# A fused attention and mixture-of-experts layer: the seam between its two halves, with a separate fp16 list of the rows and the last chunks' work reordered

## The reference

```python
xn = _layernorm(x, axis=-1)                       # x: 4 x 1024 x 256, that is 4096 rows
x  = x + attn(xn, w_attn, w_proj) + ffn(xn, ...)

# attn: causal linear attention, 16 heads of 16, chunks of 128 rows, phi = elu + 1
scores = where(mask, q_c @ k_c.T, 0)
num = scores @ v_c + q_c @ S ;  den = scores.sum(-1) + q_c @ z
S = S + k_c.T @ v_c ;  z = z + k_c.sum ;  y = num / (den + 1e-6) ;  return y @ w_proj.T

# ffn: each row goes to one of 8 experts
top_idx = argmax(xn @ gate_w.T + gate_b + expert_bias)
out = relu(xn @ w1[e] + b1[e]) @ w2[e] + b2[e]    # e = top_idx of the row
```

## Time and profile before

| | |
|---|---|
| median of 3 runs | 510.94 us (509.48 to 511.06) |
| profiled execution | 512.02 us |
| its span, first to last instruction | 510.2 us |
| mean granted TensorE clock | 0.992 |
| busy: PE, DVE, ACT, POOL | 486.4, 389.6, 280.7, 307.3 us |
| first `g1` matmul | 287.25 us from the start |

### The profile page before, as it was taken

The page is one execution under the profiler, slowest core; times in us unless marked ns, Lnnn a source line. Parts: engine busy times, 40 slices in busy tenths (PEclk is TensorE's granted clock), DMA queues, the critical chain, the costliest instruction groups (busy, mean ns, idle before and its releaser), DMA issues.

```text
span 510.2 us, 17893 instructions
## 1 busy us (share of the span) xinstructions
PE 486.4 (95%) x6293; PEld 403.4 (79%) x6293; DVE 389.6 (76%) x849; ACT 280.7 (55%) x540; POOL 307.3 (60%) x497
## 2 busy tenths in 40 slices
PE   7699999999999999999998699999999999999996
PEld 6578887788878888788877678888888888888884
DVE  3678898988989888898789177766776776776774
ACT  3447887888887878877885033333333333333330
POOL 5666888889898798878763523344344344344222
PEclk9989999999999999999999899999999999999999
DMA  8614575665665665655443512132212212210000
GB/s 260 221 44 120 182 212 168 194 190 180 201 176 169 191 195 186 200 168 183 135 148 106 188 35 75 53 90 68 66 56 65 84 53 79 74 50 28 22 17 2
DMA packets 34306, 62.91 MB, mean 123 GB/s; under 512 B 5677, under 2 KB 10030, under 8 KB 34096
## 3 DMA queue, kind: packets, MB, share of 16 engines
q1 hardware_dynamic: 29232, 49.17, 30.9%
q0 software_dynamic: 4992, 12.60, 8.2%
HBM read 51.00 MB, written 13.50 MB: 126 GB/s over the span
## 4 chain that ended last, share of the span: by engine, by line
PE 88%; DVE 3%; issue 3%; POOL 2%; ACT 2%; DMA 1%; DVEq 0%; POOLq 0%; ACTq 0%
PE ps L654 21%; PE ps L667 20%; PE ps L401 8%; PE ps L516 6%; PE ps L443 6%; PE ps L472 6%; PE ps L456 5%; PE ps L419 4%; PE ps L486 4%; PE ps L502 3%; PE ps L623 2%; PE ps L426 1%; PE ps L508 1%; PE ps L384 1%; DMA AR<-scr,AR 1%
## 5 line engine op out<-in xcount | busy, mean ns | idle before, releaser
L654 PEld LDWEIGHTS ps<-AR,W 128*128 x1872 | 131.5, 99 | 40.2 <-issue 1.2
L654 PE MATMUL ps<-AR,W 128*128 128x128 f16 x1872 | 155.9, 220 | 0.9 <-ACT AR L1216 0.9
L667 PE MATMUL ps<-W,ST 128*128 x624 | 150.5, 326 | 0.7 <-DVE ST L1057 0.7
L1225 ACT ACTIVATE ST<-ST 128x512 f16<-128x512 f32 x78 | 49.2, 630 | 104.6 <-DVE ST L1045 103.0
L1386 POOL DMA_INDIRECT out<-AR x39 | 39.8, 1021 | 106.4 <-DVE AR L1077 105.2
L1045 DVE SCALAR_TENSOR_TENSOR ST<-ps,TAs,B1S 128x512 f32<-128x512 f32 x78 | 58.4, 749 | 52.1 <-PE ps L654 49.6
L753 DVE TENSOR_TENSOR AR<-ps,CT 128x512 f32<-128x512 f32 x128 | 82.0, 684 | 3.2 <-PE ps L443 3.2
L1321 POOL TENSOR_TENSOR W<-ST,W 128x512 f16<-128x512 f32 x64 | 74.8, 1169 | 12.5 <-ACT W L1159 6.3
L1381 POOL DMA_INDIRECT AR<-scr,AR x39 | 50.1, 1285 | 31.4 <-issue 12.8
L1057 DVE SCALAR_TENSOR_TENSOR ST<-ST 128x512 f16<-128x512 f32 x78 | 53.6, 687 | 15.6 <-ACT ST L1225 15.6
L401 PE MATMUL ps<-xT,WA 128*128 128x128 f16 x768 | 48.9, 221 | 3.4 <-ACT xT L1109 3.4
(11 more groups left out here) (147 smaller groups left out, 787.0 us busy)
## 6 DMA issues: line engine op xcount, KB each, us to landing
ST<-in_w SPq DMA_DIRECT2D x128, 256.0 KB, 4.2
scr<-XR SPq DMA_DIRECT2D x32, 256.0 KB, 2.1
XR<-in_x SPq DMA_DIRECT2D x32, 128.0 KB, 4.6
AR<-in_b SPq DMA_DIRECT2D x1, 1024.0 KB, 5.3
AR<-in_wall SPq DMA_DIRECT2D x2, 388.0 KB, 4.1
AR<-scr,AR POOLq DMA_INDIRECT x39, 3.6
out<-AR POOLq DMA_INDIRECT x39
ST<-in_cst SPq DMA_DIRECT2D x1, 576.0 KB, 4.8
```

The source lines that it names most:

```text
L654: a = e.matmul(dst, W[:, off:off + 57472][:, bass.ds(place_of(s), 128)], XT16[s % 2][:, xl * 256 + k * 128:xl * 256 + (k + 1) * 128], star ...
L667: a = e.matmul(PS[4 + s % 2][:, 0:w], src[h % 4][:, fs], W[:, off:off + 57344 + w][:, bass.ds(place_of(s), w)], start=(f == 0 and w == 512 ...
L1225: e.activation(HH[h % 4], H32[h % 2], ACT.Relu).then_inc(a_hh, 1)
```

## The change

What it does:

- **A second list.** SP stores the fp16 half of every chunk (`X16`, 128 KB) to a new table `scr16` (`store_x16`), one iteration after the layernorm made it. For the first three slots (`NX0` = 3) POOL gathers from `scr16` into three buffers `X0` (`gather_x16`), and `tx` of slots 0, 1, 2 reads those. These gathers wait for the stores of `scr16`, not for those of `scr`. The full gathers from `scr` are made for all slots as before, but come behind, and wait for all 32 stores of `scr`, the last of which waits for `res(31)`. Slots 0 to 2 need them for `rest` only, slot 3 and later for `tx` as well.
- **XG** has 8 buffers, in the `XR` buffers; nothing sets them to zero any more (4 ACTIVATE on ACT, 2 MEMSET on POOL are gone).
- **DVE**: `pick_a(3)` to `ahead(3)` stand in iteration 32 behind `places(0)` and ahead of `res(28)`; then all four masks and the state of chunk 30, then the rest of the routing, with `y(29)` inside it; `to_slots` is in two halves. `s_mask(31, 1..3)`, `y(30)`, `y(31)`, `res(30)` stand behind `ids`; `res(31)` stands in slot 0 of the second half. `rest(s)` moves one slot later. `lg(31)` on ACT comes before `relu(31)`.
- **PE**: `place(3)` comes right behind `st(30)`, the 32 small matmuls right behind `pr(29)` and `warm(30)`; `inter(31)`, `yt1(30)`, `pv(31)`, `yt2(30)`, `pr(30)`, `yt1(31)` behind them. `yt2(31)` and `pr(31)` stand behind steps 3 and 5 of the second half. `warm(24)` and `warm(44)` are gone.
- **ACT** does the last eight weight quarters with `y1` and `y2` between them; `y2(29)` stands ahead of quarters 60 to 63. **POOL** waits for `v_ox` once, then does the low parts without further waits for DVE; the last stands behind `gather_x16(0)`. **SP** loads `b2` (1 MB) after `pv(31)` and ahead of the last two stores.

The core of the diff:

```diff
+        NG, NX0 = 8, 3
+        X0 = [XR[4][:, 0:256].bitcast(F16)] + [WAF[:, 512 * i:512 * i + 512] for i in range(NX0 - 1)]
...
+            def store_x16(c):
+                e.wait_ge(S["xl"], c + 1)
+                e.dma_start(scr16[c * 128:(c + 1) * 128, :], X16[c % R]).then_inc(d_s16[c % R], 16)
...
+            store_res(NC - 3)
+            e.wait_ge(S["pv"], NC)
             e.dma_start(B2, b2).then_inc(d_b2, 16)
+            store_res(NC - 2)
+            store_res(NC - 1)
...
+                if s < NX0:
+                    e.wait_ge(d_g16[s], 16)
+                    x16 = X0[s]
+                else:
+                    e.wait_ge(d_gat[s % NG], 16 * (s // NG + 1))
...
+                if t == 3:
+                    yt2(NC - 1)
+                if t == 5:
+                    pr(NC - 1)
...
+            e.wait_ge(v_ids, 1)
+            gather_x16(0)
+            w_lo(NW - 1)
+            for s in range(1, NX0):
+                gather_x16(s)
+            for c in range(NC - R, NC):
+                e.wait_ge(d_scr[c % R], 16 * (c // R + 1))
             for s in range(NG):
+                if s == NG - 1:
+                    e.wait_ge(t_tx, 1)
                 gather(s)
```

More of the change, by code:

```diff
@@ L590, in tensor @@
             st(NC - 2)
+            place(3)
             yt1(NC - 3)
             inter(NC - 2)
-            yt2(NC - 3)
             pv(NC - 2)
             scores(NC - 1)
+            yt2(NC - 3)
             pr(NC - 3)
+            warm(30)
+            for c in range(NC):
+                if c % 16 == 0:
+                    e.wait_ge(v_eq, c // 16 + 1)
+                if c % 8 == 0:
+                    e.wait_ge(v_ao, c // 8 + 1)
+                a = e.matmul(PS[1][:, 0:NS], AO[c // 8][:, :, c % 8], EQS[:, :, c], start=(c == 0), stop=(c == NC - 1))
+            a.then_inc(t_ids, 1)
             e.wait_ge(S["t32"], n_state(NC - 2))
-            warm(30)
+            inter(NC - 1)
             yt1(NC - 2)
-            place(3)
-            inter(NC - 1)
             pv(NC - 1)
@@ L1323, in gpsimd @@
             nn_begin(1)
-            for p in range(NC + 5):
+            for p in range(NC + 1):
                 if p == 0:
```

164 lines of the change are left out of this document (91 added, 73 removed).

## The result

| | before | after |
|---|---|---|
| median | 510.5 us (509.48 to 511.06, 4 runs) | 518.09 us (516.99 to 518.91, 4 runs) |
| ratio to before | 1 | 1.015, 95% interval 1.012 to 1.018 |
| profiled execution, span | 512.02, 510.2 | 517.53, 515.7 |
| mean granted clock | 0.992 | 0.980 |
| first g1, behind the start of `pr(28)` | 29.9 (287.25 - 257.33) | 31.7 (287.61 - 255.90) |

A forecast was written before the change was run, and what follows sets the result against it. PE was taken as the bound, with waits at the seam for row numbers and first gather. Mark - 0.6, stop's clock + 1.7, thin stretches + 1.5 gave + 2.6, taken as + 2.2: 513.1 us, range 509.6 to 515.8.

The forecast's parts named there:

- point (2): Sign in the changed profile: PE idles about 2.3 us twice, ahead of yt2(29) and yt2(30), released by DVE.
- The stores: First half up to iteration 32: 32 added stores of 128 KB on SP, taken at 0, at most 1 us.
- The stop at slot 3: PE waits 4.5 us ahead of slot 3's transposes for the fourth full gather; the clock's fall behind adds 1.7.
- the row's 3.6: Landing time of a gather, taken from the profile as 3.6 us; the Trainium skill's formula gave 2.6.
- Point (1): Sign at the seam: the 32 small matmuls end near 274 and the first fetch is issued near 275.8.
- Point (3): Sign at the start of the second half: first g1 at 284.0 instead of 287.25, 3.25 us won.
- Ports: POOL's low parts against DVE's routing operations: each could hold one back by up to 1.2 us; left to the rivals.
- The rival with ports: Three low parts fall into DVE's slots and places: 1.6 us more, in all + 3.8, 514.7 us; chance 0.08.
- Clock of the thin stretches: Two thin stretches of PE, 265.7 to 268.8 and 277.2 to 284, lose clock: 1.5 us together.
- From the first g1 to slot 3: Chain through res(31), its store, four full gathers and landing: slot 3's transposes 14.6 us behind the first g1.
- The mark of slot 3: Start of slot 3's transposes, behind which both kernels do the same: 298.6 instead of 299.23, 0.6 us gained.
- the rivals: Among them, late flags with both thin stretches: res(31) 6.4 us behind first g1, not 4.1; + 4 to + 5.5; chance 0.17.

The follow-up runs named there:

- e13_no_low: The changed kernel with POOL working out only 8 of 512 columns of the last seven weight quarters' low parts, the rest zeroed earlier: 515.4 us, ratio 1.0108.
- e8_last_first: The changed kernel with yt2(31), pr(31), res(31) back ahead of the second half and y(30) right behind the masks: 511.6 us, ratio 1.0036.

## Why the prediction was right and wrong

**Right.** The gather no longer bound the first g1, and PE had two more thin stretches, released by DVE's `y`, as point (2) asks. The stores were free. The stop at slot 3 was there by the same chain, with a fall of the clock behind it (mean 0.57 over 4 us, 1.7), and was worth what the sum gave it: 5.9 us by the ratios for 4.5 and 1.7. That its length came out at 4.3 for 4.5 is in part luck, because both of its ends were about 1 us late: the rows came at the first g1 plus 15.6 instead of 14.6, and PE was through at plus 11.2 instead of 10.1. Landing of the fourth gather (3.7) bore out the row's 3.6 and not the 2.6 that the prediction set beside it. The direction was right.

**Wrong.** The step that failed is the way to the first g1: contention on the ports taken at nothing, and the clock of the two thin stretches at about half of its price. Point (1) fell first: the small matmuls were to end near 274, 16.7 behind `pr(28)`, and ended 20.3 behind it, so of the 6.4 us to be won there came 2.8. Point (3), the first g1 at 284.0, 26.7 behind `pr(28)`: measured 31.7, 5.0 later, of which the terms below give 4.95. Point (2) named 2.3 us twice; it was 3.25 and 3.11.

- *Ports, taken at 0, measured 2.2.* L915 and L919 took 1.2 more together, the comparison 1.0 more. The prediction had the rule and the price ("up to 1.2" each) and set it beside the slots and places, which have cover. The low parts run from 261 on, beside the routing ahead of `y(29)`, for which PE stands idle from 264.5 on, and one stands beside the comparison, ahead of `y(30)`. Neither has cover. The rival with ports had 0.08 and the wrong place; e13_no_low shows that it deserved to be a term.
- *Clock of the thin stretches, taken at 1.5, measured 2.75.* `yt2(29)`, `pr(29)` and the idle matmuls took 0.25, 0.9 and 1.1 more than at full clock, `pr(30)` to the first g1 0.5. The reason given for 1.5 ("neither is as empty as the 3.03 us were") failed: both were 3.1 to 3.25, because DVE was late by the ports. So the two errors are in part one chain, and e13_no_low shows it: with idle times of 2.0 and 1.5 the clock fell once, for a shorter time, and not at all in front of the first slots.
- *From the first g1 to slot 3, 15.6 for 14.6.* `res(31)` at 4.7 for 4.1 (four steps of g1 with one set of transposes took 2.0 at full clock, not 1.6), the three gathers 4.3 for 3.9 (one took 1.41), the rest to the tenth.

The mark of slot 3 was to move by - 0.6 + 1.5 = 0.9; behind `pr(28)` it stands at 303.17 - 255.90 = 47.3 and stood at 299.23 - 257.33 = 41.9, so it moved by 5.4. The difference of 4.5 is 2.2 + 1.25 + 1.0. With the 1.7 behind the stop the sum is 7.1; from `pr(28)` to the transposes of slot 30 the two profiles lie 6.9 apart (197.5 and 190.6), and the medians 7.6. The clock's term and the late `res(31)` lay inside what the rivals named, the ports, with 2.2 for 1.6, outside; and the range failed because it let only one of them happen at a time.

## What to carry to other kernels

When work is cut loose from an engine and begins to run beside another's small dependent operations, price each such operation at the length of the intruder, and look first at those for which a third engine is already idle. Each idle time of 3 to 4 us in front of dense matmuls was followed by a stretch at 0.57 to 0.61 of the clock in after, so the lateness of one engine is paid twice. Shorter ones give no safety: e8_last_first had 1.3 us ahead of its first transposes and then 0.50 from 286.6 to 290.0, e13_no_low 1.5 ahead of `yt2(30)` and no fall. And when a late value feeds several transfers, put the one that is needed first at the head, and don't issue the others in a row: here the order of eight gathers was worth 1.1%, and in a kernel in which PE had gaps beside the burst, their spacing as much.
